# Maxima and squares of x taken batch by batch, and an early half weight: one change between two stages of a decoder kernel

## The reference, cut to what matters

```python
def simple_rms_norm(x, dim):
    rms = jnp.sqrt(jnp.mean(x * x, axis=-1, keepdims=True) + EPS_RMS)
    return x / rms * dim ** (-0.5)

def activation_quant(x):
    scale = 127.0 / jnp.clip(jnp.max(jnp.abs(x), axis=-1, keepdims=True), EPS_Q)
    return jnp.clip(jnp.round(x * scale), -128, 127) / scale

def weight_quant(w):
    return jnp.sign(w) * jnp.mean(jnp.abs(w))
...
    x = _layernorm(x + _L1_xattn_ref(x, ctx_1024, fside_BxSx2_0, fside_BxSx2_0, ...), axis=-1)
    x = _layernorm(x + _L1_ffn_ref(x, L1_ffn_w1, L1_ffn_b1, L1_ffn_w2, L1_ffn_b2), axis=-1)
```

## Time and profile before

| | |
|---|---|
| median of 3 runs | 2914.24 us (2910.81 to 2917.01) |
| the profiled execution's own time | 2908.72 us |
| its span, first to last instruction | 2906.9 us |
| TensorE matmul busy | 2467.0 us, 85% |
| VectorE busy | 1799.7 us, 62% |
| ScalarE busy | 1248.9 us, 43% |
| mean granted TensorE clock | 0.951 of full speed |

### The profile page before, as it was taken

One profiled execution on the slowest core, in us unless ns is written; L12 is line 12 of the kernel. 1 busy time (PEld: TensorE's weight loads), 2 busy tenths in 40 slices (PEclk: granted clock), 3 DMA queues, 4 the chain that ended last, 5 costly groups with the idle time before them and its releaser, 6 DMA issues. The chain is left out here.

```text
span 2906.9 us, 42566 instructions
## 1 busy us (share of the span) xinstructions
PE 2467.0 (85%) x15730; PEld 1904.7 (66%) x15746; DVE 1799.7 (62%) x5199; ACT 1248.9 (43%) x2982; POOL 297.7 (10%) x535
## 2 busy tenths in 40 slices
PE   5889999999974999799999999995888888883674
PEld 4668999998864999476667766763655555551332
DVE  6656767667875666445445544454566666657986
ACT  3434445444433211244344434452544444436663
POOL 3211100001000000000000000002111111101220
PEclk8999999999986999999999999997999999996887
DMA  4101211112005000000000000001000000003001
GB/s 156 62 23 41 70 37 40 69 36 74 29 26 194 1 1 1 1 1 1 1 1 1 1 1 1 1 1 51 5 5 5 5 5 5 5 1 133 1 1 58
DMA packets 41212, 83.41 MB, mean 29 GB/s; under 512 B 4528, under 2 KB 17840, under 8 KB 39856
## 3 DMA queue, kind: packets, MB, share of 16 engines
q1 hardware_dynamic: 41008, 80.70, 7.9%
HBM read 72.30 MB, written 8.39 MB: 28 GB/s over the span
## 5 line engine op out<-in xcount | busy, mean ns | idle before, releaser
L1990 DVE TENSOR_REDUCE s_nmax<-s_a_ps 128x2 f32<-128x512 f32 x256 | 174.3, 686 | 198.7 <-PE s_a_ps L1772 195.7
L651 ACT ACTIVATE s_p<-s_ms,s_nmax 128x256 f32<-128x256 f32 x256 | 128.5, 503 | 192.3 <-DVE s_nmax L754 192.3
L754 DVE CUSTOM_DVE_ANT_0 s_ms<-s_s_ps,s_bias 128x256 f32<-128x256 f32 x256 | 98.2, 421 | 175.9 <-PE s_s_ps L529 175.5
L1375 ACT ACTIVATE l_wo_w<-l_wo_w,s_nmax 128x128 f32<-128x128 f32 (+1 forms) x256 | 114.4, 447 | 197.8 <-DVE s_nmax L1471 197.0
L512 PE MATMUL s_q_ps<-s_xT,s_wh 128*128 128x256 f32 x1024 | 189.6, 286 | 0.0
L1215 PE MATMUL s_s_ps<-l_wqb_w,s_lT 128*128 128x512 f32 x384 | 175.7, 597 | 16.0 <-DVE l_wo_w L1441 15.3
L914 PE MATMUL s_h_ps<-s_xh,s_t 128*128 128x256 f32 x704 | 173.0, 284 | 9.3 <-DVE s_xl L1002 9.3
L1886 ACT ACTIVATE s_pT<-s_s_ps 128x512 f32<-128x512 f32 x256 | 151.6, 606 | 59.6 <-PE s_s_ps L1785 57.3
L562 PE MATMUL s_y_ps<-s_wh,s_oT 128*128 128x512 f32 x512 | 173.0, 399 | 0.0
L914 PE MATMUL s_h_ps<-s_xl,s_t 128*128 128x256 f32 x704 | 172.4, 283 | 0.0
L512 PEld LDWEIGHTS s_q_ps<-s_xT,s_wh 128*128 128x128 f32 x1024 | 165.5, 193 | 6.0 <-issue 0.5
(11 more groups left out here) (304 smaller groups left out, 6686.8 us busy)
## 6 DMA issues: line engine op xcount, KB each, us to landing
s_x_raw<-kept SPq DMA_DIRECT2D x24, 512.0 KB, 3.3
s_c_in<-in_ctx_T SPq DMA_DIRECT2D x32, 256.0 KB, 2.5
l_wqb_w<-in_l_xwq SPq DMA_DIRECT2D x4, 1024.0 KB, 7.8
l_wqb_w<-in_l_xwo SPq DMA_DIRECT2D x4, 1024.0 KB, 10.1
kept<-s_x_raw SPq DMA_DIRECT2D x8, 512.0 KB, 2.7
l_wo_w<-in_l_wo SPq DMA_DIRECT2D x1, 4096.0 KB, 15.5
s_raw<-in_l_w1T SPq DMA_DIRECT2D x2, 2048.0 KB, 9.9
s_raw<-in_l_w2T SPq DMA_DIRECT2D x2, 2048.0 KB, 21.5
```

The costliest lines, as they stand in the source:

```text
L651: act.activation(p[:, h % PR, q, :], ms[:, h % 2, q, :], ACT.Exp, scale=-1.0, bias=nmax[:, h % PR, q:q + 1], accum_out=den[:, h % PR, q:q ...
L754: dve.tensor_tensor_reduce(ms[:, h % 2, q, :], s_ps[:, h % 2, q * S:(q + 1) * S], bias[:, h // PER % B, :], -SCALE, 3.0e38, ALU.add, ALU.m ...
L1375: act.activation(p[:, h % PR, q, 0:(q + 1) * P], ms[:, h % 2, q, 0:(q + 1) * P], ACT.Exp, scale=-1.0, bias=nmax[:, h % PR, q:q + 1], accum ...
L1990: dve.tensor_reduce(nmax[:, g % 2, :, 2 * pair + e], a_ps[:, n % 2, :].rearrange("p (q k) -> p q k", q=QT), AX_X, ALU.max, negate=True).th ...
```

## The change

The maximum and the squares of x that stage 5 needs are taken in stage 4, a batch at a time. In step n = 28 VectorE, right behind the norm of batch b - 1, takes the maximum of its two tiles in one instruction (128 x 1024). At the end of step n = 31 ScalarE waits for that norm and squares its two tiles. For batch 7 both come in the last round, at the end of stage 4. The results go to two small tiles `of_x` that outlive the stage. Stage 5 begins with `scales` at once.

The tiles of wq, wk and wv become parts of one tile `early` of 2 MB that also outlives the stage. When the last value projection of batch 7 is done, SP loads the first half of w1 into it; stage 5 uses it as its `raw0` and loads the other three halves as before.

```diff
-def axial_attention_stage(core, wq, wk, wv, wo, bo, ctx_T, places):
+def axial_attention_stage(core, wq, wk, wv, wo, bo, ctx_T, places, early, of_x, then):
-        wq_sb = m.sb("wq", [P, DK, D])
-        wk_sb = m.sb("wk", [P, CK, D])
-        wv_sb = m.sb("wv", [P, CK, D])
+        blocks = early[:, :].rearrange("p (k n) -> p k n", n=D)
+        wq_sb, wk_sb, wv_sb = blocks[:, 0:DK, :], blocks[:, DK:DK + CK, :], blocks[:, DK + CK:DK + 2 * CK, :]
+        sq = m.sb("sq", [P, D], BF16)
...
+            sp.wait_ge(f_full, f_turns.at(B - 1, ("here", "v", QT - 1)) + 1)
+            then(sp)
...
+            def squares(b):
+                act.wait_ge(dve_steps, (b + 1) * (QT + LN_STEPS))
+                for t in range(b * QT, b * QT + QT):
+                    if t:
+                        act.wait_ge(xsq_full, t)
+                    act.activation(sq[:, :], core.x[:, t, :], ACT.Square, accum_out=of_x["squares"][:, t:t + 1]).then_inc(xsq_full, 1)
...
+                    if n == H - 1 and has(b, "prev"):
+                        squares(b - 1)
...
                         if n == LN_AT[2]:
                             scale_rows(step, dve, r, lambda q: core.x[:, (b - 1) * QT + q, :], w)
                             step.end()
+                            now = slice((b - 1) * QT, b * QT)
+                            dve.tensor_reduce(of_x["most"][:, now], core.x[:, now, :], AX_X, ALU.max,
+                                              apply_absolute_value=True)
...
-        raw = [m.sb(f"raw{n}", [P, N * P // 2]) for n in range(4)]
+        raw = [early] + [m.sb(f"raw{n}", [P, N * P // 2]) for n in range(1, 4)]
...
-            for n, (of, _, k) in enumerate(sources):
+            for n, (of, _, k) in list(enumerate(sources))[1:]:
...
-            for t in range(T):
-                if t:
-                    act.wait_ge(xsq_full, t)
-                act.activation(sq[:, 0:D], core.x[:, t, :], ACT.Square, accum_out=xs["squares"][:, t:t + 1]).then_inc(xsq_full, 1)
...
-            x_steps.done(dve.tensor_reduce(xs["most"][:, :], core.x[:, :, :], AX_X, ALU.max, apply_absolute_value=True))
-            dve.wait_ge(xsq_full, T)
             scales(x_steps, xs, D)
...
+        early = ctx.enter_context(nc.sbuf_tensor("early", [P, 2 * DK * D], F32))
+        def load_up(sp):
+            k = DK // 2
+            sp.dma_start(early[:, :].rearrange("p (k n) -> p k n", k=k), rows("l1_w1T")[:, 0:k, :]).then_inc(early_full, 16)
```

More of the change, by code:

```diff
@@ L1622, in axial_attention_stage @@
         o_out = m.sem("o_out")
+        xsq_full = m.sem("xsq_full")
         dve_steps, high_in, rden_in = m.sem("dve_steps"), m.sem("high_in"), m.sem("rden_in")
@@ L2044, in _, with quantised_ffn_stage @@
             steps_of(B)
-def quantised_ffn_stage(core, w1, b1, w2, b2):
+def quantised_ffn_stage(core, w1, b1, w2, b2, early, early_full, of_x):
     nc = core.nc
@@ L2079, in quantised_ffn_stage @@
         hqT = m.sb("hqT", [P, QT, IK, P], BF16)
-        xs = {n: m.sb("x_" + n, [P, T]) for n in ("squares", "most", "root", "tmp", "levels", "unit")}
+        xs = {n: m.sb("x_" + n, [P, T]) for n in ("root", "tmp", "levels", "unit")}
+        xs.update(of_x)
         hs = {n: m.sb("h_" + n, [P, QT]) for n in ("squares", "most", "root", "tmp", "levels", "unit")}
@@ L2088, in quantised_ffn_stage @@
         y_ps = m.ps("y", [P, 2, 512])
-        raw_full = [m.sem(f"raw_full{n}") for n in range(4)]
+        raw_full = [early_full] + [m.sem(f"raw_full{n}") for n in range(1, 4)]
         signed, mag_full, mag_ready, scaled = m.sem("signed"), m.sem("mag_full"), m.sem("mag_ready"), m.sem("scaled")
-        prep, b_full, b1_full, xsq_full, fixed = m.sem("prep"), m.sem("b_full"), m.sem("b1_full"), m.sem("xsq_full"), m.sem("fixed")
+        prep, b_full, b1_full, fixed = m.sem("prep"), m.sem("b_full"), m.sem("b1_full"), m.sem("fixed")
         xw_full, xq_full, hw_full, hq_full = m.sem("xw_full"), m.sem("xq_full"), m.sem("hw_full"), m.sem("hq_full")
@@ L2379, in round_of @@
                     last_steps.end()
-            x_steps = Steps(dve, xs_steps, SCALE_STEPS + 1)
+            x_steps = Steps(dve, xs_steps, SCALE_STEPS)
             x_steps.round(0)
-            x_steps.done(dve.tensor_reduce(xs["most"][:, :], core.x[:, :, :], AX_X, ALU.max, apply_absolute_value=True))
-            dve.wait_ge(xsq_full, T)
             scales(x_steps, xs, D)
@@ L2442, in decoder_kernel @@
                                        a["rope_sin"].rearrange("(t p) n -> p t n", p=P))
+        early = ctx.enter_context(nc.sbuf_tensor("early", [P, 2 * DK * D], F32))
+        early_full = ctx.enter_context(nc.semaphore("early_full"))
+        of_x = {n: ctx.enter_context(nc.sbuf_tensor("of_x_" + n, [P, B * QT], F32)) for n in ("squares", "most")}
+        def load_up(sp):
+            k = DK // 2
+            sp.dma_start(early[:, :].rearrange("p (k n) -> p k n", k=k), rows("l1_w1T")[:, 0:k, :]).then_inc(early_full, 16)
         axial_attention_stage(core, rows("l1_xwq"), rows("l1_xwk"), rows("l1_xwv"), rows("l1_xwo"), everywhere("l1_xbo", D),
-                              rows("ctx_T"), a["places"].rearrange("(t p) c -> p t c", p=P))
-        quantised_ffn_stage(core, rows("l1_w1T"), everywhere("l1_b1", 2048), rows("l1_w2T"), everywhere("l1_b2", D))
+                              rows("ctx_T"), a["places"].rearrange("(t p) c -> p t c", p=P), early, of_x, load_up)
+        quantised_ffn_stage(core, rows("l1_w1T"), everywhere("l1_b1", 2048), rows("l1_w2T"), everywhere("l1_b2", D),
+                            early, early_full, of_x)
         with nc.semaphore("stored") as stored, nc.Block() as block:
```

## The result

The change makes the kernel 0.19% slower: the ratio to the kernel before is 1.0019, with a 95% interval of 1.0012 to 1.0027. The medians are 2918.03 us (16 runs) against 2912.01 us (16 runs), 6.0 us apart. The difference is real, since the interval lies above 1. The ratio lies just inside the band of 0.2% that the prediction called no change; the 6.0 us between the medians are 0.21%.

What follows compares the result with a forecast made beforehand. TensorE is busy 85% of the span, but ScalarE then VectorE set stage 5's opening and VectorE paces the batch ends. -10.5 + 7.9 + 4.8 = +2.2 us on 2914.24 gives 2916 us, range 2906 to 2923.

Steps and rivals of the forecast that it cites:

- The opening, -10.5: Start of stage 5: the scales start 2.25 us after x instead of 12.76, saving 10.5 us.
- The next thing is ready: Stage 5's opening: both halves of the first weight arrive before VectorE asks, the second with 1.2 us to spare; no cost.
- VectorE's reduction in seven places, +7.9: Stage 4, after x in batches 1 to 7: each 1.21 us reduction delays what follows by 1.13 us, +7.9 us together.
- Rival A: Stage 4 batch ends: VectorE's reduction is absorbed, leaving -10.5, about 2904 us; chance 0.13, faster.
- ScalarE's squares, nothing: Stage 4 batch ends: two squares, 1.5 us, are hidden in ScalarE's idle time before the next exponential; no cost.
- Three more clock falls, +4.8: Stage 4 batch ends: TensorE's clock falls at three more of seven places, 1.6 us each, +4.8 us.
- rival B: Stage 4: the clock falls at nearly every batch end; five additional falls give +5.4, six +7.0, about 2921 us; chance 0.16.
- rival C: Stage 4: no further clock falls, -2.6, 2911.6 us, no change; chance 0.14.

Runs made afterwards that it cites:

- The change with filler: The change plus eight unread 128x256 TensorE matmuls after the scores of steps 30 and 31, in seven batches; 2906.62 us, ratio 0.9975 to before.
- the squares alone: The change with VectorE's maximum put back into stage 5's opening as one instruction over all of x, squares left in step 31; 2911.90 us, ratio 0.9992 to before.

## Why the prediction was right, and where a term was off

The forecast was no change, 2916 us, +2.2; measured were 2918.03 and +6.0, on the edge of that band. That the time itself came within 2.0 us is in part luck: 2916 was built on a median of before of 2914.24 (3 runs), and with 16 runs that is 2912.01. The miss is in the difference, 3.8 us. By its own steps:

- *The opening, -10.5.* Right: -11.1. The scales started 2.01 us after x where 2.25 were worked out, and the rest lies between TensorE's sum of the magnitudes and its first product (2.60 us before, 2.20 now).
- *The next thing is ready.* Right: no wait of VectorE on a transfer, and without the early load 3.0 and 0.4 us of it.
- *VectorE's reduction in seven places, +7.9.* Right: 1.22 us long (1.21 forecast), 1.14 on the path (1.13), TensorE's wait from 0.30 to 1.42. The change with filler gives 7.2 for all of it. Rival A, that the reduction is absorbed, is excluded by that kernel and by the one that takes it twice.
- *ScalarE's squares, nothing.* Right, shown by the squares alone.
- *Three more clock falls, +4.8.* This is the term of the sum that was mis-sized. Stage 4 lost 16.6 us, and 16.6 less 7.9 leaves 8.7 for the clock; the filler gave back 9.4. Six of the seven ends fell in the profiled execution instead of the one of before, five more, which is where rival B was said to decide. The price was also not one for each: I priced a fall from one of 3.4 us, and three of the new ones last 6.8 to 10.2. Counted by length the stage has 27 us more of half clock, eight times 3.4, for 8.7 us: an estimate of 1.1 us for each, less than the 1.6 forecast. So three was far too few and 1.6 somewhat too much. The prediction looked only at the fall at a batch end; the three other falls of before, and the wait ahead of x behind which one of the new ones began, are not in it.

So the mechanism was right and the balance came out 4 us less kind. Rival B was nearer than the forecast, in count and in time: five additional falls were to give +5.4. That the ratio still lies within 0.2% is luck, by 0.01%.

On the Trainium skill ("TensorE: Matmul & The Clock Gate"): the section "A second HAM failure mode: psum-queue depth-cycling" says that frequent short idles between groups of matmuls make the clock go up and down. The trace agrees: the eight falls of stage 4 stand behind or at the end of waits of 1.36 to 1.94 us. Its section "HAM oscillation — how this bites in real kernels" warns of longer gaps and, taken alone, would have given rival C; against it the filler kernel shows that short waits did take the clock here (41 us of half clock, 10 with the waits filled).

## What to carry to other kernels

Work moved out of an exposed opening was free here only where its engine was idle and nobody waited: the same seven reductions cost 16 us in step 28 and nothing in step 4, on an engine that is busy 62% of the span. Before moving a step, look at the few microseconds where it lands and at which wait of the bounding engine ends on that engine. A short wait of TensorE costs more than its length if it takes the clock down, and that can be tested by a few matmuls that nobody reads, placed in the wait.

## What the runs showed that I had not expected

- Extra matmuls made the kernel faster: 112 of them, of 128x256, took the change from 1.0019 to 0.9975.
- Falls inside which TensorE met another long wait lasted longer: 6.8 us at 2154.0 (a wait of 1.27) and 10.2 us at 2461.2 (1.43 and 1.08), where all four in stage 4 of before lasted 3.4. This is seen in the profiles; no run changed the second wait alone.
